# Swin-style window attention on one core: both kinds of scores of a pair issued as one group of 64-column matmuls, with the other engines' program orders moved

## The reference

```python
x = x + conv(gn(x))                                   # gn: 32 groups, mean and variance over H, W and 12 channels
# conv: roll by (-3, -3); qkv = x @ w_qkv.T; 8 x 8 windows of 7 x 7 tokens per image; 12 heads of 32
dots = einsum('bhwid,bhwjd->bhwij', q, k) * 32 ** -0.5
dots = dots + pos_emb[rel[:, :, 0], rel[:, :, 1]]     # a bias of 49 x 49, the same for all heads
dots = dots + mask                                    # last row and last column of windows only
attn = softmax(dots)
out = einsum('bhwij,bhwjd->bhwid', attn, v)
out = out @ w_out.T + b_out                           # then roll by (3, 3)
```

## Time and profile before

| | |
|---|---|
| runs | 4921.78, 4924.46, 4931.34 us |
| profiled execution: span from the first to the last instruction | 4928.9 us |
| PE busy (matmuls) | 4505.4 us, 91% |
| DVE busy | 4300.4 us, 87% |
| ACT, POOL busy | 2274.6 us, 2315.5 us |
| DMA engines, mean share busy | 37% |
| mean granted TensorE clock | 0.983 |

### The profile page before, as it was taken

The page is one execution under the profiler, slowest core; times in us unless marked ns, Lnnn a source line. Parts: engine busy times, 40 slices in busy tenths (PEclk is TensorE's granted clock), DMA queues, the critical chain, the costliest instruction groups (busy, mean ns, idle before and its releaser), DMA issues.

```text
span 4928.9 us, 186850 instructions
## 1 busy us (share of the span) xinstructions
PE 4505.4 (91%) x64564; PEld 3042.2 (62%) x64564; DVE 4300.4 (87%) x10486; ACT 2274.6 (46%) x4228; POOL 2315.5 (47%) x1936
## 2 busy tenths in 40 slices
PE   3999999999999999999999999999999999999998
PEld 2666666666666666666666666666666666666665
DVE  5988888888889889888898898898898888988887
ACT  0544444444444444444444444444444444444444
POOL 1544444444444444444444444444444444444444
PEclk9999999999999999999999999999999999999998
DMA  4433333343334333333333343343334333433332
GB/s 116 109 88 101 102 95 99 94 102 101 90 98 110 88 100 103 95 99 94 102 101 90 99 110 88 100 107 91 101 99 99 98 91 100 106 87 101 102 95 66
DMA packets 231378, 482.66 MB, mean 98 GB/s; under 512 B 39057, under 2 KB 140946, under 8 KB 222866
## 3 DMA queue, kind: packets, MB, share of 16 engines
q1 hardware_dynamic: 230722, 472.04, 37.2%
HBM read 163.61 MB, written 77.07 MB: 49 GB/s over the span
## 4 chain that ended last, share of the span: by engine, by line
PE 52%; DVE 23%; issue 20%; DVEq 2%; ACT 2%; SPq 1%; DMA 0%; POOL 0%; POOLq 0%; ACTq 0%
PE ps_pj L1038 19%; PE ps_post L1132 11%; PE ps_pj L1034 8%; PE ps_post L1123 3%; DVE lg L853 3%; DVE atl L860 3%; PE ps_sa L1072 2%; PE ps_st L1072 2%; DVE xn L805 2%; DVE mw L870 2%; DVE dev L738 2%; PE ps_pv L1114 2%; PE ps_pv L1116 2%; PE ps_pv L1115 2%; PE ps_st L1101 1%
## 5 line engine op out<-in xcount | busy, mean ns | idle before, releaser
L512 POOL TENSOR_TENSOR pl<-pf,ph 64x588 f16<-64x588 f32 x512 | 789.8, 1543 | 1872.8 <-ACT ph L624 1872.8
L554 ACT ACTIVATE qk<-ps_pj 128x392 f16<-128x392 f32 x768 | 381.7, 497 | 1045.6 <-PE ps_pj L1038 1045.6
L1038 PE MATMUL ps_pj<-xh,wh 128*128 128x392 f16 x2304 | 785.0, 341 | 5.4 <-POOL xl L487 4.6
L1038 PE MATMUL ps_pj<-xh,wl 128*128 128x392 f16 x2304 | 782.7, 340 | 0.0
L1038 PE MATMUL ps_pj<-xl,wh 128*128 128x392 f16 x2304 | 781.5, 339 | 0.0
L624 ACT ACTIVATE ph<-ps_st,sc 64x588 f16<-64x588 f32 x1024 | 771.5, 753 | 6.5
L818 DVE TENSOR_TENSOR qk<-ps_pj,qk 128x392 f16<-128x392 f32 x768 | 432.2, 563 | 314.7 <-ACT qk L554 307.5
L532 POOL TENSOR_TENSOR rb<-tq,cst 128x588 bf16<-128x588 bf16 x512 | 659.4, 1288 | 63.1 <-POOL pl L512 29.5
L487 POOL TENSOR_TENSOR xl<-xn,xh 128x392 f16<-128x392 f32 x387 | 348.2, 915 | 643.9 <-ACT xh L560 536.5
L1132 PE MATMUL ps_post<-woh,ath 128*98 128x384 f16 x1536 | 522.4, 340 | 59.0 <-DVE atl L860 50.4
L619 ACT ACTIVATE pf<-ps_st,sc 128x588 f32<-128x588 f32 x512 | 384.1, 750 | 410.1 <-PE ps_st L1072 410.1
(11 more groups left out here) (107 smaller groups left out, 10102.2 us busy)
## 6 DMA issues: line engine op xcount, KB each, us to landing
stack<-qk SPq DMA_DIRECT2D x1536, 147.0 KB, 3.7
sx<-in_x SPq DMA_DIRECT2D x69, 1176.0 KB, 8.6
xs<-in_x SPq DMA_DIRECT2D x384, 84.0 KB
out<-xb SPq DMA_DIRECT2D x384, 84.0 KB
xs<-in_x SPq DMA_DIRECT2D x384, 63.0 KB
out<-xb SPq DMA_DIRECT2D x384, 63.0 KB
xs<-in_x SPq DMA_DIRECT2D x128, 66.0 KB
out<-xb SPq DMA_DIRECT2D x128, 66.0 KB
```

Source lines behind the costliest of these rows:

```text
L512: nc.gpsimd.tensor_tensor(pl[PAD:, :, PAD:PAD + N], pf[PAD:, :, :], ph[PAD:, :, PAD:PAD + N], ALU.subtract).then_inc(s_pl[1], 1)
L1038: m = mm(ps_pj[bank][:, 0:RT].rearrange("p (w n) -> p w n", w=NW), wa[:, c, o:o + 128], xa[:, b, c, :, 0:N], **on)
```

## The change

On PE, `transposed_scores` first issues both matmuls with `rb` and then all 24 small ones, and it moves from behind the second group of units to the very start of the step, right in front of `scores`. `shift_rows` moves in front of `project_out`. On ACT, `probabilities` is cut in two: `pf` moves to the start of the step, `ph` (now `probabilities_high`) stands behind the first units and the `xh`, in front of the second units. On DVE, the low part of the first units and `atl` move behind the chain `mw`, `mt`, `mt`. POOL and SP keep their order. No instruction is added or taken away, and no buffer changes.

```diff
@@ scalar engine
             def step(n, first=False, last=False):
                 for k in range(8):
                     t = 8 * n + k
+                    if not (first and k < 1):
+                        probabilities(t - 1)
                     if not (first and k < 3):
                         attended_high(t - 3)
                     if not (last and k >= 4):
                         units(n, k, 0)
                         x_highs(n, k)
+                    if not (first and k < 1):
+                        probabilities_high(t - 1)
+                    if not (last and k >= 4):
                         units(n, k, 1)
-                    if not (first and k < 1):
-                        probabilities(t - 1)
                     shift_rows(t)
@@ probabilities is cut behind pf
                 nc.scalar.activation(pf[:, :, :].rearrange("p (a h) n -> p a (h n)", a=2), ps_st[:, :, 0:HH * N], ACT.Exp,
                                      scale=sc[:, 0:1])
+
+            def probabilities_high(t):
                 need(act, s_pv, t)
@@ vector engine
                     maxima(t, k)
-                    if not (last and k >= 4):
-                        units(n, k, 0, first)
-                    if not (first and k < 3):
-                        attended_low(t - 3)
...
                     maxima_low(t)
+                    if not (first and k < 3):
+                        attended_low(t - 3)
+                    if not (last and k >= 4):
+                        units(n, k, 0, first)
                     if not (first and k < 2):
                         invert(t - 2)
@@ tensor engine, transposed_scores
                 for hh in range(2):
-                    out = ps_st[:, hh, 0:HH * N]
-                    mm(out, bt[:, kind, :], rb[:, hh, :, :].rearrange("p h n -> p (h n)"),
+                    mm(ps_st[:, hh, 0:HH * N], bt[:, kind, :], rb[:, hh, :, :].rearrange("p h n -> p (h n)"),
                        start=True, stop=False, skip_group_check=True)
+                for hh in range(2):
                     m = score_blocks(ps_st, odd, p, hh, True, start=False, stop=True, skip_group_check=True)
                 m.then_inc(s_st, 1)
@@ tensor engine, step
                     t = 8 * n + k
+                    if not (first and k < 1):
+                        transposed_scores(t - 1, *back(n, k, 1))
                     scores(t, n, k)
                     if not (first and k < 3):
                         transpose_attended(t - 3, k - 3 + 8)
...
                     if not (last and k >= 4):
                         units(n, k, 1, last)
-                    if not (first and k < 1):
-                        transposed_scores(t - 1, *back(n, k, 1))
+                    shift_rows(t)
                     if not (first and k < 3):
                         project_out(t - 3)
-                    shift_rows(t)
```

More of the change, by code:

```diff
@@ L634, in _ @@
             end = 8 * (LAST + 1)
+            probabilities(end - 1)
             attended_high(end - 3)
-            probabilities(end - 1)
+            probabilities_high(end - 1)
             attended_high(end - 2)
@@ L1166, in _ @@
             end = 8 * (LAST + 1)
+            transposed_scores(end - 1, LAST, 7)
             transpose_attended(end - 3, 5)
             attend(end - 2, LAST, 6)
-            transposed_scores(end - 1, LAST, 7)
             project_out(end - 3)
```

## The result

The changed kernel takes 5349.89 us, the median of four runs (5346.09 to 5354.65), against 4923.12 for the kernel before on the same chip: a ratio of 1.0874, with a 95% interval of 1.0855 to 1.0892. The forecast was 5098, with a range of 4915 to 5195. The sign is right, and the loss is 427 us where 174 were forecast. The mean granted clock fell from 0.983 to 0.919; the span of the profiled execution is 5349.9 us.

The account below looks back on a forecast made before the run. PE's row of starts was taken as the bound, DVE close behind. Loop waits outweigh PE's 3.3 us saving: +0.7 us a round, plus 2.1 for the clock, +2.8, times 62 = +174 us: 5098 us, range 4915 to 5195.

Parts of the forecast that it names:

- T + 9.85: Step 2: forecast end of `rb` on POOL, counted from T, when the transposed scores start at the step's head.
- The group of 48: PE, head of a step: 48 small matmuls with their two wide ones take 1.10 us.
- The loop through POOL: From T to next T through ACT and POOL: steps 2 and 6 take 10.0 us, step 3 9.2.
- The bound for `pl`: DVE's `pl` near POOL's in steps 2, 3, 6: 1.27 us taken, 1.92 the other end, +2.0 us a round.
- The first rival: The loop through POOL doesn't bind, PE gets its 210 us: 4715 us at best, about 4850 if half; 13%.
- Step 7: Same loop (9.2 us), hidden by the pause at the border of rounds; 9.5 us taken.
- none in step 0: PE waits some 2 us for `rb` in steps 2, 3 and 6, none in 0, 1, 4 and 5.
- The clock: Three new PE waits a round, half followed by a slow stretch at 1.4 us: +2.1 us, bounds 0 and 5.1.
- The third rival: Each new PE wait is followed by a slow stretch, in step with the rounds: about 5280 us; 7%.
- Step 5: PE: gains 0.41 us and may lose its 0.66 us wait on DVE: 9.7 us for 10.77.
- The maxima: DVE's `mt` up to 1.0 us late for PE in step 2, costing nothing as ACT finishes `ph` later.
- PE saves 210 us, firm: PE: one group of small matmuls a step instead of three, 0.41 us less a step, 210 us over 512 pairs.

Follow-up runs that it names:

- Experiment 6: Changed kernel with POOL's residual behind `rb` in steps 2, 3, 6 and 7 only: 5139.34 us, ratio 1.0445 to the kernel before.
- experiment 7: Changed kernel with POOL's `rb` ahead of `pl`, residual last in steps 2, 3, 6, 7, ACT's `tq` ahead of `ph` there: 4783.22 us, ratio 0.9713.
- experiment 2: Changed kernel with 32 dummy matmuls ahead of the group in steps 3, 4 and 7: 5112.0 us, ratio 1.039 to the kernel before.
- Experiment 3: Changed kernel with 32 dummy matmuls ahead of the group in steps 0, 3, 4 and 7: 5065.36 us, ratio 1.0293 to the kernel before.
- experiment 8: Changed kernel with DVE's old order, low part of the first units and `atl` in front of the maxima: 5527.73 us, ratio 1.1237.
- experiment 9: Kernel before with both wide matmuls first and DVE's order of the changed kernel; PE, ACT, POOL keep their orders: 4859.02 us, ratio 0.987.
- experiment 1: Kernel before with both wide matmuls first in `transposed_scores`, nothing else moved: 4932.91 us, ratio 1.0024.
- experiment 10: Kernel of experiment 7 with each wide matmul again followed by its own 12 small ones: 4804.11 us, ratio 0.9774 to the kernel before.
- experiment 4: Changed kernel with POOL's residual behind `rb` in all steps: 6249.5 us, ratio 1.2695 to the kernel before.

## Why the prediction was right in sign and wrong in size

The prediction's round without the clock had the steps 0 and 1 at 19.3, then 10.0, 9.2, 8.8, 9.7, 10.0 and 9.5, together 76.5 us, and 2.1 more for the clock. Against that stand the measured 82.0. (Small slips in its sums decide nothing: the terms of T + 9.85 give 9.82, and 43 us without new slow stretches give 4968, not 4960 or 4963.)

- **The group of 48: right.** 2428.80 - 2427.70 = 1.10 us from the first wide matmul to the transposes, as worked out, and the steps 0 and 1 take 19.24 for 19.3.
- **The loop through POOL: right in place and length.** Step 2 takes 10.03 us for 10.0, step 6 10.17 for 10.0. Within it two errors cancel: `xl` starts at T + 4.24 instead of 4.5, and `rb` takes 1.50 us where 1.18 had been priced. `ph` starts at T + 4.37 for 4.7, behind `xh`, as said. The bound for `pl` (1.27 or 1.92) was met by 1.27 in step 2; its mean in the kernel is 1.33. Experiment 6 shows by the steps 2 and 6 that the loop sets them, and in experiment 7 PE's waits for `rb` go with it. The first rival (it doesn't bind) is out.
- **Step 7: wrong in its wait, right but for the clock in its time.** I let the pause at the border hide the loop (9.5 us). It takes 11.20. POOL's last row of the step (timeline of the changed kernel) is

```profile
2478.28 1.58 POOL L532 TENSOR_TENSOR rb<-tq,cst 128x588 bf16<-128x588 bf16 x1
```

  so the loop, with its slow head, takes 2479.86 - 2469.24 = 10.6 us, and the group starts another 0.58 later; whether that is a rest of the pause is open. With the slow head taken away, in experiment 2, the step takes 9.60. The fourth wait comes from here, and "none in step 0" was wrong if one counts the wait at its head.
- **The clock: the step that failed.** The prediction put "3 x 0.5 x 1.4 = +2.1 us". The price of a stretch was nearly right, 1.6 us at the head of step 3. The chance of one was wrong: not one in two, but 243 of 248. So was the number of waits, four and not three. The heads of the steps 3, 4 and 7 account for 10.67 + 10.27 + 11.20 - 9.2 - 8.8 - 9.5 = 4.6 us of the 5.5 that the round is longer than 76.5, so 2.5 more than the 2.1 priced. The stretch at the border, which the round shown before had and 26 of 61 did not, now comes each time too: the round shown took 75.74 us, the mean over 60 rounds of the kernel before is 75.29, so the average round loses another 0.45. Experiments 2 and 3 show the cause by taking the stretches away: 238 and 285 us come back. The third rival ("in step with the rounds", 5280 us, 7%) was the right case. Its mechanism was named, but five borders in ten had been taken for a chance that each new wait would have too.
- **Why nearly every wait: open.** Why the pause of 2.2 us before was followed by a slow stretch in 35 of 61 rounds, and waits of 2.0 to 2.8 us now are in nearly all, the runs don't settle. The rounds of the changed kernel are nearly all 81.9 us long, so each wait comes alike each time; that this is the reason is argued, not shown. The length of the wait alone is not it: in experiment 8, where the rounds vary from 81.8 to 86.6 us, waits of 2.3 and 2.7 us were followed by one in 31 and 46 of 62 rounds, and in experiment 9 waits of 2.0 and 2.2 us in 44 and 45 of 62. So "one in two" was not a bad rate for a wait of this length as such, and that the changed kernel stands near the other end was not to be read from the rows of before. The Trainium skill (TensorE: Matmul & The Clock Gate, HAM oscillation) tells of a kernel in which each wait, of some 3 to 5 us there, is followed by a cold start, "Every single K-tile"; the trace of the changed kernel agrees in its four places of each round, though its waits are shorter, and those of experiments 8 and 9 do not.
- **Step 5: a wait replaced.** The 0.66 us for `qk` went, as said, but 0.58 for `varb` took its place (36.8 us in 63 times over the span): 10.43 us for 9.7.
- **The maxima: right for this order only.** PE's waits in the changed kernel hold none of weight for `mt`. But "hidden by `ph`" is not the reason to rely on: experiment 8 shows that with the old order of DVE, 1.0 us later and slower, they would have cost 178 us.
- **"PE saves 210 us, firm": nearly right for PE, wrong as time.** One group a step is worth 95 and 79 us of PE's busy time (experiments 1 and 10) where 0.21 us a pair are 107. Yet experiment 1 gained nothing with one group less, and experiment 10 lost 21 us with one more. No run came near the first rival's 4715 us: even with `rb` out of the way (experiment 7) the time is 4783.
- **Missed:** `ph` of a pair also waits for `attend` of the pair before, 98.2 us in 257 times, some 0.4 us in the steps 0, 1, 4 and 5. It cost little, because those steps had room.

Added up from the forecast: 5098, with 62 x 2.5 = 155 for the stretches in the steps, 62 x 0.45 = 28 for the border's, and 62 x (5.5 - 4.6) = 56 for the steps 5 and 6 gives 5337, 13 us short of the 5350 measured. How much of the 427 us is clock can be bounded only. The sum above holds 130 + 155 + 28 = 313 for it. Experiment 3 brings back 285, of which the kernel before loses some itself (35 x 1.4 = 49, an estimate): 236. So more than half of the loss is clock by either.

## What to carry to other kernels

Moving a consumer to the head of a step turns slack into a loop: follow the loop from its start to its start, through every engine, and first move out of it what does not belong there (here `pl` and the residual in front of `rb`, which made a loss of 427 us a gain of 141). For each new wait of 2.0 to 2.8 us on TensorE, work out the time with a slow start behind every one as well as behind half of them, and give the first a good chance: waits of this length were followed by one in 31 to 62 of 62 rounds, by the place and the kernel. Before an operation is moved later, list everyone who waits for it, the buffer's next load too; experiment 4 lost 900 us to that.

## What the runs showed of the hardware

- Idle times of TensorE of 2.0 to 2.8 us were followed by the 1.2 GHz level in 243 of 248 cases in the changed kernel, but in 44 and 45 of 62 in experiment 9 and in 31 of 62 for one of 2.30 us in experiment 8. Shorter ones: 33 of 62 at 1.78 us and 10 of 62 at 1.64 us (experiment 6), none of 62 at 1.62 us (experiment 8). 32 dummy matmuls in the waits, 1.95 us of work in the one looked at, kept the clock at 2.4 GHz (mean 0.996 against 0.919), with 1.0 us of idle time left behind them.
- DVE operations of 24 elements a partition take 0.18 us while POOL is idle, and mostly 0.6 to 0.9 us while it works. In experiment 8 they fall into the time of POOL's `xl` and residual (timeline of DVE):

```profile
2421.01 0.67 DVE L876 TENSOR_TENSOR mw<-mx,cst 128x24 f32<-128x24 f32 x1
2421.71 0.82 DVE L887 CAST mt<-mw 128x24 bf16<-128x24 f32 x1
2422.57 0.92 DVE L891 TENSOR_TENSOR mt<-mw,mt 128x24 bf16<-128x24 f32 x1
```

- The middle one has a single input and suffers as well; `mx`, which also reads one tile, does not (0.77 us in the kernel before, both under POOL's work and beside an idle POOL). The Trainium skill (GPSIMD Engine Reference, Key points) names operations with two SBUF inputs, or in a 2-port mode, as those that contend with POOL; whether this one is in such a mode, no run here shows.
- DVE's `pl` (588 elements, two inputs from SBUF) takes 0.76 us while POOL is idle and 1.52 beside POOL's `pl`, both in the changed kernel. `lg`, which reads PSUM, takes the same either way: in the kernel before 131 of the 512 lie wholly under POOL's work and take 0.76 us in the median, as do the 312 beside an idle POOL.
